# Graph attention on one core: when ScalarE takes the exponential columns and the block steps, and gathers without a mid-group wait

## The reference

```
e     = leaky_relu(xl[src] + xr[dst])            # dot product q[src]*k[dst] in the others
score = einsum('ehc,hc->eh', e, att)
ex    = exp(score - segment_max(score, dst)[dst])
denom = segment_sum(ex, dst)
out   = segment_sum(xl[src] * ex, dst) / denom   # then the node's own step
```

## Time and profile before

| | us |
|---|---|
| median of 3 timed runs (7275.86 to 7287.23) | 7276.15 |
| the profiled execution itself | 7268.52 |
| its span, first to last instruction | 7266.8 |
| TensorE busy (matmul) | 4960.7 (68%) |
| VectorE busy | 5007.5 (69%) |
| ScalarE busy | 1751.7 (24%) |
| GpSimd busy | 4810.0 (66%) |
| L1018 in pass 1, first and last of 52 starts | 1225.6, 2257.7 |
| L1018 in pass 5, first and last of 52 starts | 6195.7, 7227.9 |

### The profile page before, as it was taken

One profiled execution on the slowest core, in us unless ns is written; L12 is line 12 of the kernel. 1 busy time (PEld: TensorE's weight loads), 2 busy tenths in 40 slices (PEclk: granted clock), 3 DMA queues, 4 the chain that ended last, 5 costly groups with the idle time before them and its releaser, 6 DMA issues. The chain is left out here.

```text
span 7266.8 us, 92453 instructions
## 1 busy us (share of the span) xinstructions
PE 4960.7 (68%) x26319; PEld 4144.5 (57%) x26319; DVE 5007.5 (69%) x14623; ACT 1751.7 (24%) x5241; POOL 4810.0 (66%) x5008
## 2 busy tenths in 40 slices
PE   2555555667775777777687877876777776666666
PEld 2444444666664555665466666655666665566665
DVE  4434434777775888888677777766777775788886
ACT  2334332222222222222122222221222222121111
POOL 3777776777775777776555665537666662777774
PEclk8676766777777888777777887777888887787887
DMA  4544445666664444444344444437666664666665
GB/s 132 169 159 160 159 160 157 212 212 215 212 211 124 152 150 144 144 144 137 122 143 148 147 163 132 144 106 231 222 215 206 222 217 127 217 222 224 222 222 154
DMA packets 408011, 1264.32 MB, mean 174 GB/s; under 512 B 128774, under 2 KB 189958, under 8 KB 321110
## 3 DMA queue, kind: packets, MB, share of 16 engines
q1 hardware_dynamic: 200000, 760.63, 29.1%
q0 software_dynamic: 200240, 492.90, 23.8%
q10 hardware_dynamic: 7270, 4.88, 0.2%
HBM read 1081.15 MB, written 176.88 MB: 173 GB/s over the span
## 5 line engine op out<-in xcount | busy, mean ns | idle before, releaser
L757 POOL DMA_INDIRECT gathered_rows<-table_l,arena x3056 | 2962.8, 969 | 1427.3 <-issue 877.7
L1319 PE MATMUL ps<-weighted_rows,onehot 128*128 128x136 f32 (+2 forms) x8320 | 1616.9, 352 | 903.7 <-DVE acc L1171 899.3
L1319 PEld LDWEIGHTS ps<-weighted_rows,onehot 128*128 128x128 f32 x8320 | 1416.8, 250 | 1076.5 <-DVE weighted_rows L1160 483.5
L1286 PEld LDWEIGHTS ps<-dst_side,onehot_t 128*128 128x128 f32 x8320 | 1310.3, 233 | 403.6 <-issue 318.5
L757 POOL DMA_INDIRECT gathered_rows<-table_l,src_rel_edges x1120 | 1063.6, 950 | 614.5 <-issue 314.7
L1286 PE MATMUL ps<-dst_side,onehot_t 128*128 x8320 | 1390.0, 322 | 98.9 <-DVE products L1079 50.8
L1171 DVE TENSOR_TENSOR acc<-acc,ps 128x136 f32 (+2 forms) x4160 | 1186.8, 285 | 110.0 <-PE ps L1319 28.5
L1093 DVE TENSOR_REDUCE scores<-products 128x16 f32<-128x512 f32 (+2 forms) x1040 | 709.1, 682 | 13.4
L880 PE MATMUL ps<-gathered_rows,onehot 128*128 128x128 f32 x1664 | 335.7, 364 | 487.2 <-ACT gathered_rows L817 483.7
L757 POOL DMA_INDIRECT arena<-table_l,src_rel_edges x544 | 516.4, 949 | 203.4 <-issue 154.5
L1283 PE MATMUL ps<-gathered_rows,ident 128*128 128x512 f32 x832 | 554.1, 753 | 91.7 <-DMA gathered_rows<-table_l,arena 85.9
(11 more groups left out here) (312 smaller groups left out, 6156.0 us busy)
## 6 DMA issues: line engine op xcount, KB each, us to landing
onehot_t<-onehots_turned SPq DMA_DIRECT2D x260, 1024.0 KB
onehot<-onehots SPq DMA_DIRECT2D x260, 1024.0 KB, 5.5
onehots<-onehot SPq DMA_DIRECT2D x52, 1024.0 KB
onehots_turned<-onehot_t SPq DMA_DIRECT2D x52, 1024.0 KB
table_l<-arena SPq DMA_DIRECT2D x50, 1024.0 KB
gathered_rows<-table_l,arena POOLq DMA_INDIRECT x3056, 2.5
segment_flags_sb<-segment_flags SPq DMA_DIRECT2D x1300, 8.2 KB
arena<-type_mask_rows SPq DMA_DIRECT2D x75, 256.0 KB
```

What stands on the lines that cost most here:

```text
L757: pool.indirect_dma_start(out=home(v, t // GC)[:, t % GC, :], out_offset=None, in_=table, in_offset=bass.IndirectOffsetOnAxis(ap=index[:, ...
L1286: ins = nc.tensor.matmul(ps[:, BZ + k, g * P:(g + 1) * P], e.ohT[:, u, t * P:(t + 1) * P], kRows[:, bass.ds(bs[t % 8], D)], start=not gat, ...
L1319: ins = nc.tensor.matmul(ps[:, BP + n % 3, at:at + PW], e.oh[:, u, t, :], exvT[:, t, :], start=True, stop=True)
```

## The change

Three things. GpSimd's mid-group wait (`paced`) is taken out of passes 1 to 5. ScalarE's `exp_columns` moves from the start of a slot (there for group s - 2) to the end of the slot before, after hook 6 and ahead of the pair sum 0 of the next group. And the block steps of passes 2 to 5 get later hook numbers, each step of ScalarE at least one hook after the step it waits for; AfterL1 is as it was. The mask of the next block is still loaded at -4 (pass 3) or -1 (passes 4 and 5). Core of the diff:

```
-                if t % GC == 0 and paced:
-                    paced(pool, s, t // GC)
...
-        def paced(pool, s, j):
-            if j == 2 and s >= 2:
-                e.z_ready.wait(pool, a_no, J * (s - 1) + 3)
...
             def slot(s, w, qw, cur=True, chain=True, weigh=True, ahead=True):
-                if weigh:
-                    exp_columns(s - 2)
                 if chain:
                     keep_scores(s - 1)
...
                 after.act(act, x + 6)
+                if chain:
+                    exp_columns(s - 1)
                 if cur and ahead:
                     keep_pair_sums(s + 1, 0)
                 after.act(act, x + 7)
...
 class AfterGats(Typed):
-    LAST = 22
+    LAST = 26
...
-            elif d == 3:
+            elif d == 6:
                 self.standard(dve, c, k, "std").then_inc(S["scale"], 1)
-            elif d == 5:
+            elif d == 9:
                 self.by_type(dve, k + 1, k, "q_done", k)
...
-            if d == 4:
+            if d == 8:
                 self.turn(pe, self.e.hN[:, k, :], "h_made", k, "rel_taken", BANDS * k)
-            elif d == 6:
+            elif d == 11:
                 self.key_and_value(pe, k, k + 1)
-            elif d == 7:
+            elif d == 12:
                 self.query(pe)
-            elif 8 <= d < 12:
-                self.relations(pe, k, d - 8)
+            elif d in (14, 16, 18, 20):
+                self.relations(pe, k, (d - 14) // 2)
...
@@ class AfterGats, act
-            elif d == 2:
+            elif d == 5:
                 self.deviation(act, k, "var", "std")
...
@@ class AfterTyped, act and pe
-            if d == 11:
+            if d == 14:
                 self.take_kv(act, k)
                 self.take_query(act, k)
...
-            elif d == 10:
+            elif d == 13:
                 self.key_and_value(pe, k, 2 * k + 2)
-            elif d == 11:
                 self.query(pe)
-            elif 12 <= d < 16:
-                self.relations(pe, k, d - 12)
+            elif 15 <= d < 19:
+                self.relations(pe, k, d - 15)
```

More of the change, by code:

```diff
@@ L742, in static, with gather_rows @@
     return isinstance(s, int) and s < below
-def gather_rows(nc, e, block, pass_no, table, index, home, free, free_before, here, buffers, ways, paced=None):
+def gather_rows(nc, e, block, pass_no, table, index, home, free, free_before, here, buffers, ways):
     @block.gpsimd
@@ L938, in attention_pass @@
     with after.S, nc.Block() as block:
-        def paced(pool, s, j):
-            if j == 2 and s >= 2:
-                e.z_ready.wait(pool, a_no, J * (s - 1) + 3)
-        gather_rows(nc, e, block, no, table, index, home, e.exv_ready, 1, here, buffers, ways, paced)
+        gather_rows(nc, e, block, no, table, index, home, e.exv_ready, 1, here, buffers, ways)
         flags_base = [sum(16 * (h + 1) * ((NG + 1 - u) // 2) for h in (4, 4, 1, 8, 8)[0:a_no]) for u in range(2)]
@@ L1970, in pe @@
             u = k % 2
-            if d == 4:
+            if d == 6:
                 pe.wait_ge(S["parts_made"], k + 1)
@@ L2149, in sp @@
                 self.load_mask(sp, k, 1)
-            elif d == 22:
+            elif d == 26:
                 self.write(sp, k, self.e.t3_d[0])
@@ L2187, in act @@
         for k, d in self.due(x):
-            if d == 1:
+            if d == 2:
                 act.wait_ge(S["shares"], k + 1)
                 nc.scalar.activation(self.scalars(k, 32, 2), self.scalars(k, 32, 2), ACT.Exp).then_inc(S["exp_made"], 1)
-            elif d == 2:
+            elif d == 5:
                 self.deviation(act, k, "var", "std")
-            elif d == 3:
+            elif d == 7:
                 act.wait_ge(S["scale"], k + 1)
@@ L2346, in dve @@
         for k, d in self.due(x):
-            if d == 3:
+            if d == 4:
                 self.by_type(dve, 2 * k + 1, k, "q_done", k)
-            elif d == 9:
+            elif d == 12:
                 self.by_type(dve, 2 * k + 2, k, "y_made", k + 1)
@@ L2434, in act @@
         for k, d in self.due(x):
-            if d == 9:
+            if d == 12:
                 act.wait_ge(S["turned"], 2 * k + 2)
                 nc.scalar.activation(self.hT, self.corner, ACT.Copy).then_inc(S["h_kept"], 1)
-            elif d == 11:
+            elif d == 14:
                 act.wait_ge(S["last"], k + 1)
@@ L2447, in pe @@
         for k, d in self.due(x):
-            if d == 2:
+            if d == 3:
                 self.turn(pe, self.agg, "agg_made", k, "last_kept", k)
-            elif d == 4:
+            elif d == 5:
                 self.layer_pe(pe, k, k + 1)
-            elif d == 8:
+            elif d == 11:
                 self.turn(pe, self.e.hN[:, k, :], "h_made", k, "y_taken", k + 1)
-            elif d == 10:
+            elif d == 13:
                 pe.wait_ge(S["h_kept"], k + 1)
```

37 lines of the change are left out of this document (18 added, 19 removed).

## The result

| | median us | lowest to highest | profiled span us |
|---|---|---|---|
| before | 7281.59 | 7275.86 to 7287.23 | 7266.8 |
| after | 7070.99 | 7064.91 to 7076.48 | 7063.2 |

Each median is that of four executions. The ratio is 0.9713, 95% interval 0.9699 to 0.9728: 2.9% faster. The forecast was 7090 with a range of 6985 to 7215. GpSimd's gather L757 is L755 now, and the lines from the attention pass on are 6 lower: the exponential L1018 is L1012, the column copy L1023 is L1017, the pair sum's copy L1004 is L998, the weighing L1157 is L1151.

The account below looks back on a forecast made before the run. GpSimd's gathers were taken to bound passes 1 and 5, a ring of VectorE, TensorE and ScalarE passes 2 to 4. Terms -45 - 91 + 0 - 50 = -186 us took the 7276.2 median to 7090, range 6985 to 7215.

Parts of the forecast that it names:

- The bound and the floor: GpSimd's 16 gathers allow 20.2 us a slot and bind passes 1 and 5; an engine ring holds passes 2 to 4.
- The early copy: Column copy ahead of the next pair sum's copy cuts VectorE's wait: -45 us in pass 2, between 0 and 53.
- the 60 promised: Sign: VectorE's waits for the column copy in passes 2 to 4 under 60 us together instead of 370.
- Pass 3, hook-7 blocks: Blocks starting at hook 7: gaps close and projections move into the open-node drop's idle time; -7 x 13 = -91 us.
- two floors: Floor of VectorE's idle gap ahead of the weighing, left by reading eight block numbers: 0.89 us each.
- Pass 3, hook-1 blocks: Blocks starting at hook 1: one gap goes, one of nearly the same size comes; 0 x 12, bounds 38 us either way.
- Pass 4: Later projections and relations: -20 us in hook-7 blocks, -30 in hook-1 blocks; -50 together, between 0 and 90.
- Rival C: Slower: one-piece projections of 5.7 us at hooks 4 to 6 in passes 3 and 4; +99 us, 7375; chance 0.08.
- The square root: Table switch of 1.28 us ahead of the column copy in pass 3's hook-1 blocks: no cost in the sum.
- The mid-group waits: Removing GpSimd's 270 us of waits in pass 3 gives 0, bounds -10 to +15 us; its waits move to VectorE's weighing.
- Rival B: TensorE's clock stays up with shorter idle time in passes 2 to 4: 97 us more, 6993; chance 0.13.
- The sum: -45 - 91 + 0 - 50 = -186 us over passes 2, 3 and 4.

Follow-up runs that it names:

- the last kernel: root_drop_query with pass 4's query projection one hook later in hook-1 blocks only, hook-7 blocks keeping both projections in one piece; 6932.73 us, ratio 0.9523.
- early_only: The kernel before with only the exponential-column copy moved to the slot's end; 7094.14 us, ratio 0.9754.
- gats_old: The changed kernel with pass 3's block steps put back to their old hooks; 7070.17 us, ratio 0.9724.
- root_later: The changed kernel with VectorE's use of the square root in pass 3, and what hangs on it, one hook later; 7042.41 us, ratio 0.9689.
- steps_only: The kernel before with only the later block steps, keeping the late copy and mid-group waits; 7239.34 us, ratio 0.9951.
- query_apart: The changed kernel with pass 4's query projection, and the takes and relations after it, one hook later; 7062.70 us, ratio 0.9713.
- root_drop_query: root_drop with pass 4's query projection alone one hook later (d 14), relations and takes unmoved; 6928.94 us, ratio 0.9535.
- root_drop: root_later with VectorE's open-node drop ahead of hook 2's block steps and first weighting, in all passes; 6979.14 us, ratio 0.9599.

## Why the prediction came out, step by step

**The bound and the floor: right for passes 1, 4 and 5.** Passes 1 and 5 moved by 5 us together, and slots of pass 4 came down to 20.4 only in the last kernel, where GpSimd waits for another engine no longer than its own issue. Pass 2 has a floor of its own that the working missed: its gathers are longer, 20.8 us a slot in after, and every kernel with the early copy lies at 20.7 to 21.0 there.

**The early copy: right in its place, too small in its share.** -45 in pass 2 was -53, and luck has a part in that: the measured gain is the working's most, 88.4 - 40 x 0.89, but what ended it was GpSimd, which that working did not have as a bound in pass 2. VectorE's waits for the copy in passes 2 to 4 are 0.8 + 7.4 + 67.2 = 75 us instead of 370, over the 60 promised, nearly all in pass 4. What the working missed is that the copy alone brings pass 3's hook-7 slots to their final 23.95 us. By early_only against before it is worth 57 us in pass 2, 94 in pass 3 and 26 in pass 4.

**Pass 3, hook-7 blocks: right in size, wrong in cause.** I forecast -7 us a pair of slots, from 54.6 to 47 us, because the gaps of 5.92 and 2.45 us would go (less two floors they are 6.6 us, not the 6.7 of the working) and the projections would move into the drop's idle time. The pair went from 54.1 on average to 47.9 us, 80 us over 13 blocks where I had 91. But the step that gave all of it to the projections' move failed: early_only leaves them where they were and reaches 47.9 too. The late copy was about half of the gap. The projections' part was real and smaller, the 34.9 us that early_only still waits; the change took these away, and the wait for the square root, 38.6 us, stands in their place. So the moves show 12 us (gats_old against after) and 34 us once that wait is gone too (gats_old 23.95, root_later 23.29). By early_only the slot fell by 3.1 us where the gap ahead of the weighing, averaged over these slots, fell by 2.0 (4.2 to 2.2), and in hook-1 slots by 0.55 where the gap fell by 2.2: a gap is a poor guide to a phase. The granted clock differs between the two in the same sense: it rose from 0.76 to 0.88 in the hook-7 slots and from 0.85 to 0.87 in the others. That it made up the 1.1 us beyond the gap fits and is not shown.

**Pass 3, hook-1 blocks: right within its bounds.** 50.2 us a pair became 48.4, -22 us over 12 blocks where I had 0 (bounds 38 either way). Without the early copy the same steps cost 1.9 us a slot (steps_only), 3.9 a pair, more than the positive bound of 3.2: that cost is not seen beside the early copy.

**Pass 4: right in sign, -71 instead of -50.** The copy gives 26 of it and the steps about 1.8 us in each hook-7 slot (22.71 in early_only, 20.87 after). I had the larger gain at the hook-1 blocks, and there the projections ahead of the turning back, and behind them the last take at the hook of the next block's turn, cost what query_apart and root_drop_query got back: 1.7 and 3.0 us a slot. Rival C's mechanism was thus there in one pass and one phase, at a small part of its price, and together with a lower clock.

**What I left out.** The square root. I priced its table load in hook-1 blocks alone, where it stands ahead of the column copy, and not that in hook-7 blocks VectorE would wait for it at d 6: 38.6 us in 13 waits, of which root_later got 22 back. The producer moved by three hooks (2 to 5) and so did its consumer (3 to 6), but at the new place ScalarE's queue stood behind a wait of 9.33 us.

**The mid-group waits: right.** 0 alone and 0 beside the rest, with GpSimd's waits moved to the weighing as promised.

**Rival B, the clock: present, its share open.** In pass 3 the granted clock went from 0.80 (3535 to 4845 of before) to 0.86 without any fill, that is, more of the pass ran at the upper of the two levels, 1.2 and 2.4 GHz. Two kernels that raised it by another 0.07 and 0.08 gained 0.11 and 0.23 us a slot, but their extra products held the drop up by 1.2 us, so these are not the clock's worth. Against them stand the hook-1 slots of pass 4, where a pair of slots of after takes 45.5 us at 0.79 and 41.1 at 0.92. The total stayed by the forecast and far from the rival's 6993; how much of the -210 came through the clock, above all in pass 3's hook-7 slots, no run separates. The rule of the Trainium skill that I cited ("TensorE: Matmul & The Clock Gate", Part 1), that idleness halves the rate and work restores it, agrees with 0.86 to 0.93. In the stretch before the drop in after's pass 3 TensorE worked 1.22 of 4.80 us, and the 5.60 us behind it ran at 0.55, nearly all at the lower level:

```profile
3707.30:3712.10 4.80, 1.22 (x6) 0.92 (x5) 4.44 (x19) 0.00 (x0) 3.58 (x5) 0.50 0.20 55
3712.20:3717.80 5.60, 5.60 (x16) 3.91 (x16) 4.59 (x11) 0.75 (x2) 4.38 (x5) 0.55 0.18 50
```

**The sum.** -186 forecast, -203.6 by the spans and -210.6 by the medians: I was 8 short in pass 2, 13 in pass 3 and 21 in pass 4, and had at nothing the 5 that passes 1 and 5 grew by and the 19.5 around the passes, which the later steps cost. That the total came within 20 us of the forecast is in part luck: the three passes were 42 short together, and 24.5 were left out the other way. The medians differ by 7 more than the spans because the profiled execution of before, 7268.5, lay under its median.

**Still open.** Pass 3 stands at 22.2 to 22.3 us in the best kernels, 2 above the 20.2 us of pass 1. What closes its ring now was not tested; TensorE's waits for VectorE's additions (93.2 us in 80 in root_drop) are the largest left. Pass 2's gathers are slower than pass 1's (797.36 us for 800 in after, 0.997 each, against 767.31 for 805, 0.953), and why was not tested either. A kernel that holds the clock up without delaying the drop, and one that keeps pass 4's order at either clock, would tell what the clock is worth.

## What to carry to other kernels

A copy that one engine waits for belongs directly behind the instruction that makes it ready, ahead of any copy that still has to wait for a third engine: that one line gave 176 of 210 us here. When steps are spread over later slots, it is not enough to move the consumer of each step as far as its producer: look at what the producer's queue waits for at the new place, and check that the last step of one item still precedes the first of the next that waits for it. A small operation for which an idle engine waits goes in front of block work, not behind it; two lines moved on VectorE were worth 63 us after the other edits (7042.41 to 6979.14).

## What the hardware showed that was not expected

- The granted clock of a pass rose from 0.87 to 0.95 with ten extra products of 128 columns a slot (970.62 to 1024.50 us of TensorE busy time in 1180 us), and the pass gained 11 us, with the drop held up by 1.2 us more a slot. Work that fills an idle stretch to keep the clock up is itself in the way when the wait ends.
- The same order of work ran at two paces in one execution: two slots of pass 4 in after took 45.5 us at a granted clock of 0.79 and the next two 41.1 at 0.92, with TensorE busy 37.59 and 32.51 us.
- A square root between two exponentials costs ScalarE two loads of 1.28 us, with the activation 0.01 us behind the first (3718.62 + 1.28, then 3719.91) and the second load 0.02 us behind its end (3719.91 + 0.20, then 3720.13). The draining of 1.38 us that the Trainium skill gives ("ScalarE: Activation LUTs", What ACT_TABLE_LOAD costs) is seen behind neither, nor ahead of the first, which starts 0.02 us after the activation before it (3717.94 + 0.66, then 3718.62).
- GpSimd's gathers stand 1.26 us apart in passes 1 and 4 of the last kernel, and can run ahead enough for 13 slots of 19.6 us on average where 16 gathers need 20.2.
